# An audio tower on one core: where tiles begin in SBUF, and how rows of x are padded

## The reference

```python
for i in range(3):                       # three state-space layers
    dbc = einsum('ble,ce->blc', x, W_dbc[i])
    delta, Bm, Cm = split(dbc, [1, 65])
    delta = softplus(delta * W_dt[i] + b_dt[i])
    h[t] = exp(delta * A) * h[t - 1] + (delta * x) * Bm      # scan over time
    x = einsum('blen,bln->ble', h, Cm) + D[i] * x
    if i < 2: x = mean of neighbouring steps                 # 375 -> 187 -> 93
h = x
h = h + attention(layernorm(h))          # 8 heads, second order kernel
h = h + experts(layernorm(h))            # top 2 of 6, three layers each
```

## Time and profile before

| | us |
|---|---|
| median of 3 runs | 646.61 |
| lowest and highest | 645.93, 646.9 |
| the profiled execution | 645.23 |
| its span, first to last instruction | 643.5 |
| PE busy | 567.3 |
| DVE, ACT, POOL busy | 526.0, 513.3, 436.6 |

### The profile page before, as it was taken

One profiled execution on the slowest core, in us unless ns is written; L12 is line 12 of the kernel. 1 busy time (PEld: TensorE's weight loads), 2 busy tenths in 40 slices (PEclk: granted clock), 3 DMA queues, 4 the chain that ended last, 5 costly groups with the idle time before them and its releaser, 6 DMA issues.

```text
span 643.5 us, 22845 instructions
## 1 busy us (share of the span) xinstructions
PE 567.3 (88%) x9531; PEld 297.8 (46%) x9531; DVE 526.0 (82%) x924; ACT 513.3 (80%) x1044; POOL 436.6 (68%) x597
## 2 busy tenths in 40 slices
PE   2666777899999999999899999999999999989993
PEld 1232323555454545555454455555555544545441
DVE  5898899999979898988888888989898887654342
ACT  1334558889988999999888897999989887878781
POOL 7747799888777877876776777688785866423120
PEclk9986579999999999999999999999999999999997
DMA  3432232132121222122021222131310100000001
GB/s 73 80 83 52 61 69 63 41 66 53 38 56 26 62 59 51 32 57 57 21 63 42 61 45 61 38 68 31 66 23 21 27 20 14 21 14 8 9 13 29
DMA packets 77574, 28.51 MB, mean 44 GB/s; under 512 B 69271, under 2 KB 77463, under 8 KB 77463
## 3 DMA queue, kind: packets, MB, share of 16 engines
q1 hardware_dynamic: 71290, 25.92, 18.7%
q10 hardware_dynamic: 6173, 1.05, 1.0%
HBM read 13.25 MB, written 3.05 MB: 25 GB/s over the span
## 4 chain that ended last, share of the span: by engine, by line
PE 53%; DVE 16%; ACT 15%; POOL 5%; DMA 4%; issue 4%; ACTq 2%; SPq 2%; DVEq 0%; POOLq 0%
PE ring L1267 8%; PE ring L1346 5%; PE ring L1359 5%; PE ring L1454 4%; PE ring L1253 4%; PE ring L1425 3%; PE ring L1434 3%; ACT pm L1050 2%; DVE ring L1716 2%; PE ring L1242 2%; PE ring L1336 2%; PE ring L1222 2%; PE ring L1405 2%; PE ring L1329 1%; DMA x_D<-x_D 1%
## 5 line engine op out<-in xcount | busy, mean ns | idle before, releaser
L1050 ACT ACTIVATE pm<-ring 93x744 f32<-93x744 f32 x128 | 96.3, 782 | 10.8 <-PE ring L1346 9.9
L1346 PE MATMUL ring<-q_exp,qk 32*93 32x372 f32 x512 | 56.2, 507 | 7.5 <-POOL q_exp L894 1.0
L1844 DVE TENSOR_TENSOR hidw<-hid,ring 128x744 f32<-128x744 f32 x48 | 44.3, 923 | 17.8 <-PE ring L1415 13.2
L1359 PE MATMUL ring<-pm,v 97*32 97x93 f32 x2048 | 53.5, 245 | 1.3 <-DVE base_A L1720 0.6
L1093 ACT ACTIVATE hid<-ring,b_col 128x372 f32<-128x372 f32 x96 | 49.4, 568 | 4.2 <-PE ring L1434 3.2
L894 POOL TENSOR_TENSOR q_exp<-qk,mask_q 128x1488 f32<-128x1488 f32 x16 | 43.0, 2685 | 10.1 <-DVE qk L1774 10.1
L1359 PEld LDWEIGHTS ring<-pm,v 97*32 97x32 f32 x2048 | 41.7, 109 | 16.0 <-ACT pm L1050 3.0
L1100 ACT ACTIVATE hid<-ring,b_col 128x744 f32<-128x744 f32 x48 | 42.2, 879 | 7.8 <-PE ring L1425 5.5
L879 POOL TENSOR_TENSOR base_C<-base_C,carry_C 128x744 f32<-128x744 f32 x16 | 28.4, 1777 | 27.0 <-DVE carry_C L1725 19.0
L1425 PE MATMUL ring<-hid,w 64*64 64x372 f32 x384 | 40.2, 488 | 0.6 <-ACT rows_hi_D L974 0.2
L1434 PE MATMUL ring<-nrm_f,w 64*64 64x372 f32 x384 | 39.5, 485 | 0.0
(11 more groups left out here) (366 smaller groups left out, 1753.4 us busy)
## 6 DMA issues: line engine op xcount, KB each, us to landing
xin_A<-in_x_dram SPq DMA_DIRECT2D x62, 93.0 KB
xin_B<-in_x_dram SPq DMA_DIRECT2D x62, 93.0 KB
x_A<-x_A SPq DMA_DIRECT2D x32, 93.0 KB, 3.0
x_B<-x_B SPq DMA_DIRECT2D x32, 93.0 KB, 3.0
x_C<-x_C SPq DMA_DIRECT2D x32, 93.0 KB, 2.2
out_dram<-osb SPq DMA_DIRECT2D x15, 186.0 KB
x_D<-x_D SPq DMA_DIRECT2D x32, 46.5 KB, 1.9
w<-in_L_ffn_expert_w_dram SPq DMA_DIRECT2D x6, 48.0 KB
```

The costliest lines, as they stand in the source:

```text
L1050: a.activation(pm[q % 2][h][0:TOUT].rearrange("m a j n -> m a (j n)"), out_of(f"att.s{q}{h}", g)[0:TOUT, :, 0:COLS], ACT.Square, bias=2.0, ...
L1346: ins = mm(o[h][0:TOUT, b, 0:COLS], qk[r:r + 32, 1, q * TOUT:(q + 1) * TOUT], q_exp[r:r + 32, q].rearrange("p j n -> p (j n)"), start=True ...
L1359: ins = mm(o[32 * j:32 * j + 32, 0, h * TOUT:h * TOUT + TOUT], rows[:, at:at + 32], pm[q % 2][h][:, b, j, :], start=(b == 0), stop=(b == 1 ...
L1844: tt(hidw[k][:], hid2[:], out_of(f"ffn.g_{k}", g)[:, :, 0:COLS], ALU.mult).then_inc(me, 1)
```

## The change

A tile that a transfer writes or reads is made by `lined` instead of `sb`: it begins at a multiple of 64 bytes, for which a gap tile of 32 bytes is put ahead where needed. This is done for decay, xin, x, y_rec, attT, fin, hidw and osb. (A line is 32 bytes here, an even line begins at a multiple of 64.) The rows of x are padded from 1,488 to 1,536 bytes (D: 744 to 768); the padding is neither written nor read, and a swap still moves 1,488 (D: 744) bytes. Since rows 0 and 1 no longer touch, the step `pooled` of C writes x_D as 2 rows of 186 instead of 372 in a row; those of A and B write one row as before.

| tile | begins, past an even line: before, after | row 1 of x (a swap's source) past a 256-byte block: before, after | row 2 (its target): before, after |
|---|---|---|---|
| xin_A, xin_B | 32, 0 | | |
| x_A | 32, 0 | 240, 64 | 192, 64 |
| x_B | 32, 0 | 112, 64 | 64, 64 |
| x_C | 32, 0 | 240, 64 | 192, 64 |
| x_D | 32, 0 | 136, 64 | 112, 64 |
| decay, hidw0, hidw2, y_rec, attT | 32, 0 | | |
| fin, hidw1, osb | 0, 0 | | |

All tiles behind decay move: by 32 bytes up to x_A, by 480 behind x_D, by up to 640 at the end. So tiles that no transfer touches may change from an even line to an odd one or back; base_A goes from even to odd, base_B from odd to even. On every engine the instructions, their order and their waits are the same.

```diff
+        LINE, GRAIN = 64, 32
+        laid = [0]
+
         def sb(name, shape, dt=F32):
+            laid[0] += -(-prod(shape[1:]) * {F32: 4, BF16: 2, I32: 4}[dt] // GRAIN) * GRAIN
             return ctx.enter_context(nc.sbuf_tensor(name, shape, dt))
+
+        def lined(name, shape, dt=F32):
+
+            if laid[0] % LINE:
+                sb(f"{name}_gap", [P, GRAIN // 4])
+            return sb(name, shape, dt)
...
-        decay = sb("decay", [P, LAYERS, NS])
+        decay = lined("decay", [P, LAYERS, NS])
...
-        xin = {u: sb(f"xin_{u}", [XP, 2, XJ, 2, E]) for u in "AB"}
-        xs = {u: sb(f"x_{u}", [P, 3, WIDE[u]]) for u in UNITS}
+        xin = {u: lined(f"xin_{u}", [XP, 2, XJ, 2, E]) for u in "AB"}
+        xs = {u: lined(f"x_{u}", [P, 3, -(-WIDE[u] // 16) * 16])[:, :, 0:WIDE[u]] for u in UNITS}
...
-        y_rec = sb("y_rec", [P, 2 * TOUT])
-        attT = sb("attT", [P, NPAIR, 2, TOUT])
+        y_rec = lined("y_rec", [P, 2 * TOUT])
+        attT = lined("attT", [P, NPAIR, 2, TOUT])
...
-        fin = sb("fin", [P, COLS])
+        fin = lined("fin", [P, COLS])
...
-        hidw = [sb(f"hidw{k}", [P, 2, COLS]) for k in range(NEP)]
+        hidw = [lined(f"hidw{k}", [P, 2, COLS]) for k in range(NEP)]
...
-        osb = sb("osb", [TOUT, GB, E])
+        osb = lined("osb", [TOUT, GB, E])
...
-                    pairs = base[u][:].rearrange("p (t two) -> p t two", two=2)
-                    to_cols = xs[to][:, 0:2].rearrange("p b c -> p (b c)")
-                    at = COLS if u == "B" else 0
-                    g.tensor_tensor(to_cols[:, at:at + COLS], pairs[:, :, 0], pairs[:, :, 1], ALU.add).then_inc(me, 1)
+                    if u == "C":
+                        to_cols, pairs = xs[to][:, 0:2], base[u][:].rearrange("p (b t two) -> p b t two", b=2, two=2)
+                        g.tensor_tensor(to_cols, pairs[:, :, :, 0], pairs[:, :, :, 1], ALU.add).then_inc(me, 1)
+                    else:
+                        to_cols, pairs = xs[to][:, "AB".index(u)], base[u][:].rearrange("p (t two) -> p t two", two=2)
+                        g.tensor_tensor(to_cols, pairs[:, :, 0], pairs[:, :, 1], ALU.add).then_inc(me, 1)
```

More of the change, by code:

```diff
@@ L16 @@
 from contextlib import ExitStack
+from math import prod
 import concourse.bass as bass
```

## The result

| | before | after |
|---|---|---|
| median, lowest, highest us (6 runs each, side by side) | 646.03, 644.96, 646.9 | 641.51, 640.6, 643.81 |
| ratio, 95% interval | | 0.9935, 0.9914 to 0.9956 |
| the profiled execution, its span | 645.23, 643.5 | 640.64, 638.9 |

The change makes the kernel 0.65% faster, 4.2 us by the ratio (2.8 to 5.6). The forecast, 646.7 in 644.0 to 648.3, was wrong.

The account below looks back on a forecast made before the run. The prediction took PE to bound the kernel, with nearly all swaps hidden. From 645.23 us it added 0 for swaps, 0 for loads, 0.1 for engine work, then 1.4 to reach the runs' median: 646.7 us, range 644.0 to 648.3.

Parts of the forecast that it names:

- What bounds the kernel: PE, busy 88% of the span and 97.05 of 100 us between 400 and 500 us; nearly all swaps hidden.
- The swaps, taken at 0: Swaps of x on the chain: bounds +0.15 to -1.0 us from the new row positions, taken at 0.
- an odd start shows no penalty: Reason for 0 on the swaps: packets of x_A, x_B and x_D took 95, 102 and 52 ns before.
- The Trainium skill's rule that the prediction cites: Descriptors starting off a 256-byte boundary are fetched from the boundary below: 9% on x_A and x_C, about -0.2 us.
- Engine work, 0.1 us: Moved tiles cost engines nothing; POOL's two-row sum into x_D about +10 ns on 807, under 0.1 us in total.
- The loads, "I take 0": Loads of x into xin: bounds nothing to 1.0 us a group, at most -3.0 us on the chain; taken at 0.
- It counts in only three places of the chain: Loads count only ahead of a swap: x_C at 52 us, SP's stretch at 59 us, x_D at 396 us.
- The three named places: x_C at 52 us, SP's stretch at 59 us, x_D at 396 us: together at most -3.0 us from faster loads.
- Half lines do cost: Rival, chance 0.24: a half line at each end of loaded pieces costs; without them 643.7 us.
- One more swap behind instruction loading: Rival, chance 0.14: one more swap on the chain caught behind an instruction packet, 1.6 us slower, 648.3 us.
- The sign to be wrong by, a share of 16%: Wrong if the DMA queue's 18.7% falls to 16% and long landings at 52 and 65 us shrink by over 1 us.

Follow-up runs that it names:

- xin_only: Kernel before with only xin_A and xin_B moved by 32 bytes to begin on an even line: 640.74 us against 644.72, ratio 0.9937.
- shift32: Kernel before with one gap of 32 bytes ahead of decay, so every tile behind changes between even and odd lines: 640.16 us, ratio 0.9932.
- xin_odd: Changed kernel with xin put on an odd line again, 96 bytes past a block of 256: 639.56 us against 644.72, ratio 0.9924.
- xin_256: Changed kernel with xin at a multiple of 256 bytes instead of 64 past one: 639.79 us, ratio 0.9933.
- later_even: Kernel before with later groups' loads to xin on an even line, the first group's to separate tiles 160 past a block: 640.98 us, ratio 0.9944.
- xin_96: Kernel before with xin alone moved by 64 bytes, to 96 past a block, still an odd line: 639.71 us, ratio 0.9926.
- x_128: Changed kernel with all rows of x 128 past a block of 256 instead of 64: 639.73 us, ratio 0.9927.
- x_only: Kernel before with only x on even lines, its rows padded, and the two-row sum into x_D: 644.56 us, ratio 0.9997.
- rest_only: Kernel before with only decay, y_rec, attT, hidw and osb moved by 32 bytes: 645.53 us, ratio 1.0015.
- xin_32: Changed kernel with xin alone back at 32 bytes past a block of 256: 644.94 us against 644.77, ratio 1.0.
- apart_32: Kernel before with every second load transfer from group 1 on sent to spare tiles, also 32 past a block: 644.25 us, ratio 0.9993.
- xin_16: Kernel before with xin 16 bytes past a block of 256: 651.77 us against 644.27, ratio 1.0113.
- x_to_160: Changed kernel with wider rows of x, so a swap's target lies 160 past a block and its source stays at 64: 639.33 us, one run.
- x_from_160: Changed kernel with wider rows of x, so a swap's source lies 160 past a block and its target stays at 64: 637.63 us, one run.
- sweep: Kernel before with longer xin tiles, each group loaded to another start, 0 to 240 bytes past a block: 642.7 us, one run.
- first_even: Kernel before with only the first group's loads sent to separate tiles on an even line, later ones to the old xin: 643.85 us, ratio 0.9986.

## Why the prediction was wrong

All 18 profiles have the same packets on the queue, so its share on the page times 16 times the span, the time of all its packets, sorts the kernels. Beside it stands the mean of a load's packets over whole loads:

| xin past a block | kernels | queue, us | ns a packet of a load | ratios |
|---|---|---|---|---|
| 0, 64, 96, 160 | after, xin_only, shift32, xin_odd, xin_256, later_even, xin_96, x_128 | 1,806 to 1,832 | 18.0 to 18.1 | 0.9924 to 0.9944 |
| 32 | before, x_only, rest_only, xin_32, apart_32 | 1,922 to 1,946 | 20.2 to 20.3 | 0.9993 to 1.0015 |
| 16 | xin_16 | 2,091 | 24.0 | 1.0113 |

The queue's time holds the swaps too, whose packets average 95 to 101 ns in these kernels, so that the means on the right tell the price better: 2.2 ns at 32, 5.9 at 16.

The two single runs, x_to_160 (639.33 us) and x_from_160 (637.63), have queues of 1,826 and 1,852 us and 18.1 ns a packet. sweep, with mixed starts, has 1,867 us, 19.2 ns and one run of 642.7 us; first_even, nearly all at 32, has 1,912 us and 20.1 ns.

**What bounds the kernel: right.** PE's 97.05 us of the earlier trace rows are 96.98 after.

**The swaps, taken at 0: right** (x_only, 0.9997), and for them so was "an odd start shows no penalty". The Trainium skill's rule that the prediction cites, by which x_A's and x_C's packets should have shortened by 9%, is not borne out: over all swaps x_A's grew from 96.1 to 98.5 ns and x_C's from 94.0 to 99.1.

**Engine work, 0.1 us: right** (807 and 809 ns).

**The loads, "I take 0": the step that failed**, by two errors. The first is the price. The rows that I set against each other, 20.3 and 16.8 ns, did show a real difference, with 18 as the true other end, and I explained it away by the traffic beside the weights. Over whole loads it measured 20.2 against 18.1 ns. What it makes of a load I had as at most 1.0 us. Read from the traces, from the first issue of a load to the end of its last packet, the mean over the loads after the first group is 8.0 us with xin at 32, 7.4 in the kernels of the first row and 8.8 in xin_16: 0.6 us a load, in the middle of my bounds.

The second is the count. "It counts in only three places of the chain" left out the start. For the five profiles with xin at 32 (the kernel before among them, at 0) and seven without slow packets (the first seven of the table's first row) I took when matching instructions of DVE, ACT, POOL and SP start, relative to the kernel before, as a median over the 10 us from each time given, and then the mean over each set:

| us | 20 | 30 | 50 | 70 | 100 | 300 | 350 | 400 | 600 |
|---|---|---|---|---|---|---|---|---|---|
| xin at 32 | 0.0 | -0.6 | 0.7 | 0.2 | 0.0 | 0.0 | -0.1 | -0.5 | -1.0 |
| no slow packets | -1.7 | -3.0 | -2.3 | -3.4 | -3.3 | -3.3 | -3.5 | -4.5 | -5.0 |
| difference | -1.7 | -2.4 | -3.0 | -3.6 | -3.4 | -3.3 | -3.4 | -4.0 | -4.0 |

The single profiles scatter: at 30 us from 0.1 to -1.6 in the first set and from -2.9 to -3.1 in the second, at 600 us from 0 to -2.0 and from -3.3 to -6.0. So the lead at 30 us is in all seven profiles (x_128, outside the sets, has 1.6 us of it), and the later steps only in the means.

By the means some 2.4 us are made in the first 30, where the loads of two groups and the weights follow each other on SP's and ACT's queues with nothing to hide behind: all that stands behind them in the queue, weights too, lands earlier. About 1.2 us more are made up to 70 us, half of it ahead of the swap of x_C at 52 us and half around it and the stretch at 59 us, which the prediction named; then nothing for 250 us, then 0.6 at the x_D swap of 396 us that it named too. The sum, 4.0, is the measured 4.2 within its interval. The three named places show 1.2 of their bound of 3.0 in this account.

These parts don't stand alone, though. first_even, with the first group's loads fast and the rest slow, is 2.9 us ahead at 30 us and 0.5 at 50: the slow loads ahead of the swap of x_C, a place that the prediction named, took nearly all of it back, and its timed gain is 0.9 us and not 2.4. So it seems that the start's gain is kept only if the next loads are fast as well. The same profile ends 4.4 us ahead of the kernel before, which its 12 runs don't bear out, so the late part of a single profile tells little. No run has a slow first group and fast loads behind it. What is shown is that the loads give the whole of the gain, and that by 30 us there is a lead that none of the three named places can have made; how the gain splits between the start and these places stays open.

**The rivals.** "Half lines do cost" gave 643.7, the nearest of my numbers, with the wrong mechanism: xin_odd and xin_96 keep the half lines and are fast. "One more swap behind instruction loading" did not show: the longest landing of x_D on the chain is 3.30 us, against 3.58. The sign to be wrong by, a share of 16%, was set too far: the share fell to 17.9% and the kernel was faster all the same, since 2.1 ns of 20.2 on each piece is all it took.

## What to carry to other kernels

Look where small pieces that a transfer writes fall in blocks of 256 bytes of SBUF, not only at even or odd lines: in this kernel a piece of 256 bytes should start at 0 or at 64 to 192 past a block; 32 and 48 off one cost some, 16 off one costs most. One gap tile settles it. A transfer that is hidden in the steady state can still count at the start, where loads queue up ahead of the first work: look there at every load, not only at those on the chain that ended last. When you read a packet's time, take whole transfers, since here the price came only in their later part. When an experiment puts something "back", compare addresses and not their parity.

## What was not expected of the hardware

- Loads of 256-byte pieces into SBUF took 18.0 to 18.1 ns a packet over whole loads when the cut at a block of 256 left 64 bytes or more, or none, 19.2 to 20.9 ns when it left 32 or 48 bytes, and 23.2 to 24.3 ns at 16 (a single load without slow packets read up to 18.5). Head and tail cost alike.
- The price builds up within a load: in the kernel before its quarters read 18.0, 19.0, 21.6 and 22.1 ns. It needs no other piece in the same block (apart_32, 20.3 ns). Its cause is open.
- A load was carried by four DMA engines (four closing packets a transfer, against 16 for a swap), so 2 ns on a packet made 0.6 us on a load of 1,488 packets, not a sixteenth of the packet time.
- Swaps of 1,488 bytes inside SBUF don't show it: 100 to 104 ns for x_A's pair whichever end was moved off the 16 bytes.
- The total went with the packet time of the queue: 95 to 119 us less of it came with some 4 to 5 us less, 166 us more with 7.3 us more.
